# One exp per key tile over two PSUM tensors, the softmax epilogue's copy queued early, and the output writes on ScalarE's queue

## The reference

```python
def _L0_attn_ref(x, kernel, WO):
    q = jnp.einsum('bsm,hmd->bhsd', x, kernel[0])
    k = jnp.einsum('bsm,hmd->bhsd', x, kernel[1])
    v = jnp.einsum('bsm,hmd->bhsd', x, kernel[2])
    scores = jnp.einsum('bhsd,bhtd->bhst', q, k) * (1.0 / (d * d * h))
    attn = jax.nn.softmax(scores, axis=-1)
    out = jnp.einsum('bhst,bhtd->bhsd', attn, v)
    out = jnp.transpose(out, (0, 2, 3, 1)).reshape(b, s, d * h)
    return jnp.einsum('bsf,fm->bsm', out, WO[0])

def _reference_tuple_inner(x, W_r, W_k, W_v, mu_r, mu_k):      # ffn
    x_prev = jnp.concatenate([jnp.zeros((B, 1, C)), x[:, :-1, :]], axis=1)
    xr = mu_r * x + (1.0 - mu_r) * x_prev
    xk = mu_k * x + (1.0 - mu_k) * x_prev
    r = jax.nn.sigmoid(jnp.einsum('btc,dc->btd', xr, W_r))
    k_act = jnp.square(jax.nn.relu(jnp.einsum('btc,dc->btd', xk, W_k)))
    return r * jnp.einsum('btc,dc->btd', k_act, W_v)

x = _layernorm(x + _L0_attn_ref(x, ...))
x = _layernorm(x + _L0_ffn_ref(x, ...))
```

## Time and profile before

| | |
|---|---|
| median of 3 runs | 3636.78 us (3635.08 to 3708.96) |
| profiled execution | 3661.0 us; span of its slowest core 3659.3 us |
| spans of the 8 cores | 3613.5 to 3659.3 us |
| mean granted TensorE clock (share of 2.4 GHz) | 0.752 to 0.768 |
| PE busy | 2491.2 us, 68% of the span, 10176 matmuls |
| PE weight loads | 777.6 us, 21% |
| DVE busy | 834.9 us, 23% |
| ACT busy | 1213.1 us, 33%, 937 instructions |
| chain of work that ended last | PE 56%, ACT 25%, DMA 7%, issue 6%, DVE 5% |
| PE in attention: scores / values / denominators | 509.6 / 501.8 / 484.7 us |
| output DMAs | 32 of 512 KB, median 2.8 us from issue to landing |

### The profile page before, as it was taken

How to read it: one execution, slowest core, us unless ns; L and a number is a source line. 1 busy time by engine, 2 the same in 40 slices (tenths; PEclk the granted TensorE clock), 3 DMA queues, 4 the chain that set the end, 5 groups by cost and what they waited for, 6 DMA issues and landing times.

```text
span 3659.3 us, 28585 instructions; the slowest of 8 cores (3613.5 to 3659.3 us)
## 1 busy us (share of the span) xinstructions
PE 2491.2 (68%) x10176; PEld 777.6 (21%) x10176; DVE 834.9 (23%) x1369; ACT 1213.1 (33%) x937; POOL 20.1 (1%) x27
## 2 busy tenths in 40 slices
PE   0077766767767776767768777677777677767755
PEld 0033211212222221212223222121212122212212
DVE  0022000230313032302163012040123213230335
ACT  0000444344334433453300443434443443344311
POOL 0000000000000000000000000000000000000000
PEclk9977675867677787778678886676878687867767
DMA  9922000000210022001122013000120013000201
GB/s 184 203 51 59 22 0 0 24 0 23 75 52 1 23 58 69 1 0 64 51 46 46 23 46 81 1 23 0 46 81 24 0 35 93 24 1 23 92 23 46
DMA packets 85123, 157.13 MB, mean 43 GB/s; under 512 B 1984, under 2 KB 16384, under 8 KB 84992
## 3 DMA queue, kind: packets, MB, share of 16 engines
q1 hardware_dynamic: 61968, 123.84, 10.4%
q0 software_dynamic: 23024, 31.47, 5.8%
HBM read 155.31 MB, written 31.46 MB: 51 GB/s over the span
## 4 chain that ended last, share of the span: by engine, by line
PE 56%; ACT 25%; DMA 7%; issue 6%; DVE 5%; ACTq 1%; DVEq 0%; POOL 0%; another core or an unknown queue 0%; SPq 0%; POOLq 0%
PE psg L99 25%; ACT pb L109 21%; PE psab L99 11%; PE pspv L99 10%; PE psden L99 10%; ACT lta L109 3%; DMA ws<-wts 3%; DMA wsc<-ws 2%; DMA aba<-xT 2%; DVE rg L118 1%; DVE xka L118 1%; ACT rsb L109 1%; DVE aba L118 1%; ACTq L84 1%; DVE outb L118 1%
## 5 line engine op out<-in xcount | busy, mean ns | idle before, releaser
L109 ACT ACTIVATE pb<-psab 128x2048 bf16<-128x2048 f32 (+1 forms) x520 | 960.0, 1846 | 1414.9 <-PE psab L99 1228.1
L99 PE MATMUL psab<-qtb,ktb 64*128 64x512 bf16 x2048 | 509.6, 475 | 756.8 <-ACT pb L109 697.1
L99 PE MATMUL pspv<-pb,vtb 128*64 128x512 bf16 x2048 | 501.8, 498 | 27.8 <-DVE aba L118 27.8
L99 PE MATMUL psden<-pb,cstb 128*32 128x512 bf16 x2048 | 484.7, 482 | 0.0
L99 PE MATMUL psg<-xra,ws 128*128 128x512 bf16 x1320 | 402.1, 465 | 0.0
L118 DVE TENSOR_TENSOR aba<-pspv,rsb 128x512 bf16<-128x512 f32 x64 | 44.2, 691 | 1484.0 <-ACT rsb L109 1484.0
L99 PEld LDWEIGHTS psab<-qtb,ktb 64*128 64x128 bf16 x2048 | 118.8, 97 | 1136.1 <-issue 1136.1
L99 PE MATMUL psg<-aba,ws 128*128 128x512 bf16 x632 | 173.5, 434 | 245.0 <-DMA ws<-wsc 190.9
L99 PEld LDWEIGHTS pspv<-pb,vtb 128*64 128x64 bf16 x2048 | 118.8, 115 | 375.0 <-issue 374.7
L99 PEld LDWEIGHTS psg<-xra,ws 128*128 128x128 bf16 x1320 | 139.7, 114 | 246.4 <-issue 171.6
L99 PEld LDWEIGHTS psden<-pb,cstb 128*32 128x32 bf16 x2048 | 96.0, 96 | 316.5 <-issue 316.5
(11 more groups left out here) (97 smaller groups left out, 1542.9 us busy)
## 6 DMA issues: line engine op xcount, KB each, us to landing
ws<-wsc SPq DMA_DIRECT2D x36, 2048.0 KB, 9.8
ws<-wts POOLq DMA_DIRECT2D x8, 2048.0 KB, 25.8
y<-xT SPq DMA_DIRECT2D x8, 2048.0 KB, 12.0
outT<-outb SPq DMA_DIRECT2D x32, 512.0 KB, 2.8
wsc<-ws SPq DMA_DIRECT2D x7, 2048.0 KB, 12.6
aba<-xT POOLq DMA_DIRECT2D x8, 1024.0 KB, 9.1
xra<-xT POOLq DMA_DIRECT2D x6, 1024.0 KB, 9.5
cstf<-cst SPq DMA_DIRECT2D x1, 96.0 KB, 2.3
```

The lines of the kernel that those rows point to most:

```text
L99: i = e.matmul(_o, _l, _r, start=_st, stop=_sp, tile_position=_tp, skip_group_check=True)
L109: i = e.activation(_o, _i, _f, scale=_s, bias=_b)
```

## The change

Three things are changed.

1. SAB is split into two PSUM tensors SA and SB2 of 128 x 1024. Step g writes its scores into SA (g even) or SB2 (g odd), and every step has an exp of its own over 1024 columns into one slot of PB.
2. The copy to RSB (ACT) and the multiply into ABA (DVE) are emitted in `flush_pv` right behind the reciprocal of the head pair, not in `emit_epi`. The broadcast matmul on PE is still issued in `emit_epi`, two flushes later. The copy waits for that matmul (`nrb_res`).
3. In `emit_ln2_tail` the four output DMAs and their waits for `naps[i]` are on ACT's queue instead of SP's. The load of x stays on SP.

```diff
-        SAB = pst("psab", [128, 2048])
+        SA = pst("psa", [128, 1024])
+        SB2 = pst("psb", [128, 1024])
@@ emit_ln2_tail
-                    wait("s", c_va, naps[i])
+                    wait("a", c_va, naps[i])
                     out_done[0] = dma(
-                        "s",
+                        "a",
@@ emit_scores_exp
-                    so = (g % 2) * 1024
+                    sps = SA if (g % 2 == 0) else SB2
...
-                    mm(SAB[:, so:so + 512], ka, qa, True, True, tp=(0, 0))
-                    nsc = mm(SAB[:, so + 512:so + 1024], kb, qb, True, True,
-                             tp=(64, 0), inc=c_sc)
-                    loc = g % (NHP * NKT)
-                    if loc == 0 or loc == NHP * NKT - 1:
-                        pbs = PB[:, (g % PBS) * 1024:(g % PBS) * 1024 + 1024]
-                        ...
-                        npp = act(pbs, SAB[:, so:so + 1024], AF.Exp,
-                                  scale=SCALE, inc=c_p)
-                        exp_hist[g] = npp
-                    elif loc % 2 == 0:
-                        ...
-                        npp = act(
-                            bass.AP(PB, s1,
-                                    [[PBS * 1024, 128], [s0 - s1, 2], [1, 1024]]),
-                            SAB[:, 0:2048], AF.Exp, scale=SCALE, inc=c_p)
-                        exp_hist[g - 1] = exp_hist[g] = npp
+                    mm(sps[:, 0:512], ka, qa, True, True, tp=(0, 0))
+                    nsc = mm(sps[:, 512:1024], kb, qb, True, True, tp=(64, 0),
+                             inc=c_sc)
+                    pbs = PB[:, (g % PBS) * 1024:(g % PBS) * 1024 + 1024]
+                    wait("a", c_sc, nsc)
+                    if g - PBS >= 0:
+                        wait("a", c_kt, g - PBS + 1)
+                    npp = act(pbs, sps[:, 0:1024], AF.Exp, scale=SCALE, inc=c_p)
+                    exp_hist[g] = npp
@@ emit_epi: the lines from here on are taken out
-                    wait("a", c_rb, nrb_res)
-                    ncp = act(RSB[:, :], b.ap[:, :], AF.Copy, inc=c_ar)
-                    b.free = (c_ar, ncp)
-                    wait("v", c_ar, ncp)
-                    nao = vop("tensor_tensor",
-                              (ABA[:, hp_ * QT:(hp_ + 1) * QT], PV[:, :],
-                               RSB[:, :], ALU.mult), inc=c_ao)
-                    bPV.free = (c_ao, nao)
@@ flush_pv, behind the reciprocal: the same lines are put in
+                        wait("a", c_rb, nrb_res)
+                        ncp = act(RSB[:, :], b.ap[:, :], AF.Copy, inc=c_ar)
+                        b.free = (c_ar, ncp)
+                        wait("v", c_ar, ncp)
+                        nao = vop("tensor_tensor",
+                                  (ABA[:, hp * QT:(hp + 1) * QT], PV[:, :],
+                                   RSB[:, :], ALU.mult), inc=c_ao)
+                        bPV.free = (c_ao, nao)
```

More of the change, by code:

```diff
@@ L789, in emit_scores_exp @@
                     kb = KTB[64:128, hp * S + kt * 128: hp * S + (kt + 1) * 128]
-                    mm(SAB[:, so:so + 512], ka, qa, True, True, tp=(0, 0))
-                    nsc = mm(SAB[:, so + 512:so + 1024], kb, qb, True, True,
-                             tp=(64, 0), inc=c_sc)
-                    loc = g % (NHP * NKT)
-                    if loc == 0 or loc == NHP * NKT - 1:
-                        pbs = PB[:, (g % PBS) * 1024:(g % PBS) * 1024 + 1024]
-                        wait("a", c_sc, nsc)
-                        if g - PBS >= 0:
-                            wait("a", c_kt, g - PBS + 1)
-                        npp = act(pbs, SAB[:, so:so + 1024], AF.Exp,
-                                  scale=SCALE, inc=c_p)
-                        exp_hist[g] = npp
-                    elif loc % 2 == 0:
[L803 to L807, removed]
-                        npp = act(
-                            bass.AP(PB, s1,
-                                    [[PBS * 1024, 128], [s0 - s1, 2], [1, 1024]]),
-                            SAB[:, 0:2048], AF.Exp, scale=SCALE, inc=c_p)
-                        exp_hist[g - 1] = exp_hist[g] = npp
+                    mm(sps[:, 0:512], ka, qa, True, True, tp=(0, 0))
[7 more added lines that the diff above has]
+                    exp_hist[g] = npp
                     gkt[0] += 1
@@ L823, in emit_epi @@
                 def emit_epi():
-                    nrc, nrb_res, b, hp_ = att["epi"]
+                    nrc, nrb_res, b = att["epi"]
                     att["epi"] = None
@@ L887, in flush_pv @@
                         last_nrb[0] = nrb_res
-                        att["epi"] = (nrc, nrb_res, b, hp)
+                        att["epi"] = (nrc, nrb_res, b)
                         att["epi_cd"] = 1
+                        wait("a", c_rb, nrb_res)
[6 more added lines that the diff above has]
+                        bPV.free = (c_ao, nao)
                 for hp in range(NHP):
```

## The result

The changed kernel is faster, and by more than was forecast. Where the kernel before takes 3636.5 us, the median of ten executions is 2821.9 us (2765.6 to 2991.4), and the ratio is 0.7603 (95% interval 0.7578 to 0.7627). The forecast was 3070 us (2920 to 3380).

A forecast was written before the change was run, and what follows sets the result against it. PE and ACT were taken to take turns around the wide exp, neither full. Savings of 493 us in seven later attentions and 92.5 in the first, less 14 for DMAs, gave 3090, by factor 0.9934 3070 us (2920 to 3380).

The forecast's parts named there:

- tiles of a stage: Attention's 128 key tiles per stage: 1.02 us each, ACT's narrow exp, 130.6 us; floor PE's 0.98.
- boundary at full clock: Head-pair boundary: exps, Ln, broadcast, copy and PE's owed matmuls cost 4.6 us, at 64 places.
- low clock after boundaries, a stage: After each head-pair boundary: some five tiles at 1.2 GHz and a slower broadcast, 3.5 us (ends 0 and 7).
- idle beside r fillers: Later attentions, FFN r groups: PE idles 1.1 us behind ACT's chain and exp, eight times, 8.8 us.
- fillers of a later stage: Projection, FFN and layer-norm matmuls among later attention tiles: no longer under the exp, they add 69.3 us per attention.
- vector queue of a later stage: Layer-norm vector work ahead of head pair 1's multiply, 4 us late; with other chains 8 us an attention (0 to 20).
- later stage, sum: Each of the seven later attentions: 281.5 us in all, 70.4 less than 351.9.
- output DMAs: Output projection's first add to OUTB waits for DMAs issued at attention's end: 2 us, seven times 14.
- The low clock did not stay: Rival, attention stages: PE stays at the low clock, a later attention takes 400 us, kernel 3965; chance 0.06.
- The limit on the fully used chip: Rival, whole kernel: dense cores hold a die at 0.81 of the clock, 3415 us, half of it 3240; chance 0.14.
- the boundary eats more: Rival, head-pair boundaries: 8 us rather than 4.6, or vector queue 20; 302 us more, 3370; chance 0.08.
- a tile near 1.8 us: Rival, pair loop: short exps or semaphores cost more, a tile stays near 1.8 us, kernel near 3640; chance 0.03.

The follow-up runs named there:

- e3: Changed kernel with ten full-size matmuls of no use added on PE at each head-pair boundary; ratio 0.7577 to the kernel before.
- e1: Changed kernel with the third edit undone, output DMAs and their waits back on SP's queue; ratio 0.7636 to the kernel before.
- e7: Changed kernel with the ones (denominator) matmuls of key tiles 1 to 14 left out, only to measure; 2692.1 us.
- e5: Changed kernel with DVE copying PV to SBUF at each head pair's end, no ACT copy to RSB, only tile 0 put off; 2713.8 us.
- e8: Changed kernel with PV copied out at each head pair's end by ACT into RSB, ahead of Ln, DVE only multiplying; 2580.0 us, ratio 0.7079.

## Why the prediction was wrong

The direction, the mechanism and its place held: the wide exp over both halves of SAB made the engines take turns, the split ended that, and the gain lies in the attention stages. The forecast put the profiled execution at 3090; it was 2767. The gap of 323 us is made of mis-sized terms, nearly all too high. The values of a later stage are those of the second one:

| term, us | forecast | measured, from |
|---|---|---|
| tiles of a stage | 128 × 1.02 = 130.6 | 128 × 0.98 = 125.4, timeline after |
| boundary at full clock | 8 × 4.6 = 36.8 | 8 × 4.4 = 35.2 by the plain ones of e3; less where a filler runs in its wait |
| low clock after boundaries, a stage | 8 × 3.5 = 28 | first stage 9.6, after less e3; a later one about 14, an estimate |
| idle beside r fillers | 8 × 1.1 = 8.8 | 9.6, timeline after |
| fillers of a later stage | 69.3 | 67.4, a k or v pair being 3.56 and not 3.8 |
| vector queue of a later stage | 8 | 3.9, seen at one place |
| later stage, sum | 281.5 | 244.6 |
| first stage, sum | 208.7 | 181.7 |
| output DMAs | 14 in all | 0, e1 |
| ahead of the first exp | unchanged | 23.8 less |

The estimate for the low clock: in the second stage 40.3 us were granted 0.50, PE is busy in 33.9 of them, and a tile takes 1.65 us there instead of 0.98, so that each us of work loses 0.41. (The same working gives 12.3 us for the first stage, where 9.6 were measured, so it is high rather than low.) The measured values don't simply add: 125.4 + 67.4 + 35.2 + 14 + 9.6 + 3.9 = 255.5, against the 244.2 us of the second stage's window. Part of the difference is that fillers now run in the wait of a boundary: at the seven boundaries between the stage's first and last reciprocal PE idles 15.3 us, and seven plain ones have 7 × 2.89 = 20.2. The rest is not told apart. The gap is 7 × 36.9 = 258 in the later stages, 27 in the first, 14 at the DMAs and 24 ahead of the attention.

**The largest error is the low clock: 28 − 9.6 us in the first stage, and with the estimate of 13 to 19 for each of the later ones about 107 of the 323 us.** The step in the prediction said that a tile at 1.2 GHz loses 0.63 us and gave each boundary some five of them, which is 8 us at 1.65 each. That the clock falls there is right, and so is the loss of a tile. The length was wrong: in the first stage the clock was low for 34.1 of the 178 us, 4.9 us a boundary, three tiles and not five. By the prediction's own 0.63 us a tile that makes 13 us for the seven boundaries, where the sum has 28 for eight. The smaller part, from 13 down to 9.6, is that some of the low stretch covers work or waiting that delays nobody: PE idles in 3.7 of the 34.1 us, until Ln, Exp, copy and exp are through. The other end of the range (3.5 down to 0) was named and would have given 2866 with everything else kept.

**A tile is PE's 0.98, not ACT's 1.02.** The prediction took the length of a narrow exp as if successive exps could not overlap. In e7 they start 0.90 us apart while each is recorded with 1.06. The Trainium skill (ScalarE: Activation LUTs, What ACT_TABLE_LOAD costs) has this: back-to-back ACTIVATEs overlap by about 93 ns. The earlier trace rows agrees and had it already: of the three steps of 0.60, 0.72 and 0.63 us the third had 0.10 us to go when the exp behind it started. In e7 the overlap is larger, 0.16 us in the rows shown.

**The idle time beside the r fillers was right, though not place by place.** The prediction let the scores of one tile wait for an exp that stands behind the sigmoid's chain, 1.1 us each time. At two of the eight places of the second stage there is no such wait:

```profile
643.84 0.60 ACT L109 ACTIVATE lta<-psg 128x512 f32<-128x512 f32 x1
...
645.14 1.90 PE L99 MATMUL psg<-xra,ws 128*128 128x512 bf16 x8
645.88 1.01 ACT L109 ACTIVATE pb<-psa 128x1024 bf16<-128x1024 f32 x1
...
647.03 0.39 PE L99 MATMUL psa<-qtb,ktb 64*128 64x512 bf16 x2
```

The chain runs from 643.84, and the exp behind it starts at 645.88, in the middle of PE's next filler. Two tiles and a filler take 3.91 us from one filler to the next, where their matmuls make 3.86. The late fillers also go out every second step and not every third, since they catch up what the boundary held back, and so cover ACT's chain with more matmuls than the sum had. At the other six places the wait is there (the first three that are not at a boundary):

```profile
649.73 1.01 ACT L109 ACTIVATE pb<-psa 128x1024 bf16<-128x1024 f32 x1
...
650.88 0.39 PE L99 MATMUL psa<-qtb,ktb 64*128 64x512 bf16 x2 [1.82 <-ACT pb L109]
...
658.53 0.39 PE L99 MATMUL psb<-qtb,ktb 64*128 64x512 bf16 x2 [1.21 <-ACT pb L109]
...
665.08 0.39 PE L99 MATMUL psa<-qtb,ktb 64*128 64x512 bf16 x2 [1.71 <-ACT pb L109]
```

With 1.88 and 1.27 us at two further places, and 2.09 at the boundary at 673.00 where 0.34 is usual, PE idles 9.6 us, against 8.8 in the sum. That the two are so close is in part luck: six waits of 1.2 to 1.9 us, not eight of 1.1. So PE binds a tile in a plain stretch, and ACT's queue binds most of those beside the sigmoid.

**The plain boundary was right**, 4.4 us at full clock against 4.6, and so was the vector queue ahead of head pair 1's multiply, forecast as 4 us late:

```profile
615.35 0.69 DVE L118 TENSOR_TENSOR aba<-pspv,rsb 128x512 bf16<-128x512 f32 x1 [0.17 <-DVE xka L118]
...
616.18 1.06 PE L99 MATMUL pspv<-pb,vtb 128*64 128x512 bf16 x4 [3.86 <-DVE aba L118]
```

**The rivals.** The low clock did not stay: a later stage is granted 0.89 to 0.92 where before it had 0.72 to 0.76. The limit on the fully used chip was not met in the profiled execution: every core was granted 1.00 or 0.50 and none 0.81, and in e3 all eight were granted 1.00 over 169 us with PE busy 160 to 162 of them. By the rule that the prediction cites (the Trainium skill, TensorE: Matmul & The Clock Gate, Part 1) a die stays lowered under such a load. These two traces do not agree; the trace of the kernel before has the 0.81, but from 200 to 336 us only cores 0 and 1 were held at 0.73 and 0.74, while cores 2 and 3 of the same die had 0.90. That the boundary eats more did not come about, nor did a tile near 1.8 us. All four rivals and the unclear terms lay on the slow side, and only 0.04 was left below 2920. The sum had taken the upper value for the exp, the clock, the fillers and the DMAs at once. The ends on the other side that the text names (0.98 a tile, nothing for low clock, vector queue and DMAs) make 3090 − 41 − 224 − 56 − 14 = 2755, or 2737 by the factor to the median; the range should have reached down to them.

## What to carry to other kernels

When two engines take turns on one PSUM buffer, give each its half, and price the result by the busier engine's work on each tile; here that was exact to 0.01 us in plain stretches, and not where ACT had other work in its queue. Before pricing a low clock, find out how long it lasts; then count only the work of the engine within it that something waits for. Once the main loop is overlapped, look for the accumulator that an epilogue holds: copying it out first, on an engine whose queue is short, was worth another 7%, and the same copy on the engine with long chains only 2%.

## What the runs showed of the hardware that was not expected

Successive exps of 128x1024 start 0.90 to 0.92 us apart although each is recorded with 1.00 to 1.14 us (e7). Attention matmuls, which use half of the array's rows or a quarter or half of its columns, hold the full clock as well as dense projections do, once they come without gaps: 1.00 over the whole first stage in e5 and e8, and the first stage before the change, with PE busy 69% of it, was granted 0.64. Nearly 30% less attention work on PE (e7) lowered its granted clock from 0.89 to 0.86. A clock of 0.81 can take two cores of a die and leave the other two (before, cores 0 and 1 from 336 to 367 us, where cores 2 and 3 had 0.97 and 1.00).
